# Reciprocal roots of a gated-attention and mixture-of-experts block: ten linked VectorE operations or one GpSimd power

## The chip, the core and the metric

The kernel runs on one core of one Trainium2 chip. A core has five engines that run their own instruction streams and meet through semaphores: TensorE (PE in the profile; its weight loads are shown apart as PEld), VectorE (DVE), ScalarE (ACT), GpSimd (POOL) and SyncE (SP). The metric is the device time of one execution in microseconds (us), as a median over runs; lower is better.

## What is computed

One adaptive-layernorm transformer layer over 4 x 1024 tokens of width 128. The parts with a reciprocal root are three: the first and second layernorm, the norm of every head's key (16 heads of 8), and the layernorm of the attention's output. Cut from the reference:

```python
def _layernorm(x, axis=-1, eps=1e-05):
    m = jnp.mean(x, axis=axis, keepdims=True)
    v = jnp.var(x, axis=axis, keepdims=True)
    return (x - m) / jnp.sqrt(v + eps)

# attention (h is the modulated first norm)
q = _silu(x @ Wq.T); k = _silu(x @ Wk.T); v = _silu(x @ Wv.T)
f = jax.nn.log_sigmoid(x @ Wf.T)
k = k / jnp.maximum(jnp.linalg.norm(k, axis=-1, keepdims=True), EPS_NORM)
# per token: S = exp(f) * S + k (outer) v ; o = q . S
o = o * gate
var = jnp.mean(xc * xc, axis=-1, keepdims=True)
o = xc / jnp.sqrt(var + EPS_LN) * ln_w
# whole layer
h = _layernorm(x) * (1 + ca) + sa
x = x + ga * attention(h)
h = _layernorm(x) * (1 + cb) + sb
x = x + gb * ffn(h)     # 2 shared experts, and 2 of 8 chosen per token
```

## The kernel before

Every engine's instruction stream is written out by hand. The 4096 tokens are worked in NB = 8 blocks of TB = 512, each four tiles of 128 tokens. A `first_period`, seven `period(i)` and a `drain` form a pipeline: in period i, block i is scanned, block i+1 is projected, block i-1 gets its attention output, block i-2 its second norm, router and first shared-expert product, and block i-3 the rest of the shared experts and the scatter of its rows to the experts' regions in DRAM. After the drain come 71 tiles of routed rows (about 300 to 410 us of the span) and the weighted sum.

What stands around the change, engine by engine:

- DVE carries the recurrence: for each of 8 value positions v a product `update` (line 1500) into PSUM and a `scan` (line 1513) over 512 tokens. Between them stand the statistics, the router's choice (`choose`, `mark`, `targets`), the products of the experts and, once per period, `roots`.
- `roots(n, a, z, ...)` (lines 1543 to 1552) takes the reciprocal root of up to 92 columns at once: 64 head norms of block i+1 (`clamp_norms`, line 1534), 4 output variances of block i-1 (`o_variance`, line 1541), 4 second-norm variances of block i-2 (`variance_2`, line 1590) and, in the first two calls, first-norm variances of later blocks. `rsqrt` (lines 63 to 76) does it in ten operations from a bit trick and two polynomial steps; `Chain` makes each one wait for the one before it.
- Who waits for `roots`: `offset_2` (line 1594), and through it ACT's `normalise_x2` (line 999) and PE's transposes (line 643) of block i-2; ACT's `widen_norms` (line 992), and through it the keys of block i+1 (`normalise_k`, line 1563); DVE's `residual` (line 1571), and through it `statistics_2`.
- The first two blocks' first norms take their roots in `statistics_1` at the start (lines 1385 to 1393).
- POOL works its stream in order: `query` (line 1221, seven products a block), the low halves of split operands (`split_h`, `split_v`, `split_h2`, lines 1204, 1209, 1214; `split_w13`, line 1263), `gain_w2` (line 1271, four products, in period 2), and eight indirect DMAs a block (`scatter`, line 1243). An operation that waits holds up all that stand behind it.

Of the kernel before, what the change touches and what calls it, by code (L numbers as in the profile page):

```python
# [36 lines left out]
P = 128  # L37
# [25 lines left out]
def rsqrt(dve, link, y, x, t, s):  # L63


    link(dve.tensor_scalar(t.bitcast(I32), x.bitcast(I32), 1, None, ALU.logical_shift_right))
    link(dve.tensor_scalar(y.bitcast(I32), t.bitcast(I32), -1, RSQRT_SEED, ALU.mult, ALU.add))
    link(dve.tensor_tensor(t, x, y, ALU.mult))
    link(dve.scalar_tensor_tensor(t, t, -0.5, y, ALU.mult, ALU.mult))
    link(dve.scalar_tensor_tensor(y, t, 1.5, y, ALU.add, ALU.mult))  # L70

    link(dve.tensor_tensor(t, x, y, ALU.mult))
    link(dve.tensor_tensor(t, t, y, ALU.mult))
    link(dve.tensor_scalar(s, t, 0.375, -1.25, ALU.mult, ALU.add))
    link(dve.tensor_tensor(t, t, s, ALU.mult))
    link(dve.scalar_tensor_tensor(y, t, 1.875, y, ALU.add, ALU.mult))


RSQRT_STEPS = 10
# [7 lines left out]
def build(nc, x, cmod, attw, wg12, w13T, w2T, bias, consts, ids, tiles, pads, H, out):  # L87
# [28 lines left out]
    with ExitStack() as ctx:  # L116
# [55 lines left out]
        tmp1 = sb("tmp1", [P, NB * NT])  # L172
# [16 lines left out]
        rtmp = sb("rtmp", [P, NSQ + NLATE])  # L189
# [76 lines left out]
        x_sq, t_sq, lg, pos, found, mu = parts(ybank, NSQ + NLATE, NSQ + NLATE, NT * NEXP, (NT + 1) * NEXP, NT * 8, NT)  # L266
        x_sq_end, t_sq_end, mu_end = parts(obank, NSQ, NSQ, NT)
# [18 lines left out]
        s_st1 = sem("s_st1")  # L286
        s_xn1 = sem("s_xn1")
# [27 lines left out]
        s_rs = sem("s_rs")  # L315
        s_x2 = sem("s_x2")
# [185 lines left out]
        def _(pe):  # L502
# [57 lines left out]
            def k_norms(b):  # L560
                wait(pe, s_ksq, b + 1)
                wait(pe, s_rs, RSQRT_STEPS * b)
                wait(pe, s_tgt, TGT_STEPS * (b - 3))
                wait(pe, s_var2, b - 2)
# [51 lines left out]
            def means(b, chains, routed):  # L616


                sq, _, mean = squares(b)
                wait(pe, s_og, b + 1)  # L620
                if b < NB - 1:
                    wait(pe, s_rs, RSQRT_STEPS * chains)
                    wait(pe, s_var2, b)
                    wait(pe, s_tgt, TGT_STEPS * (b - 1))
                    wait(pe, s_rt, RT_STEPS * routed)
# [3 lines left out]
                for t in range(NT):  # L629
                    ins = pe.matmul(sq[:, NT * H + t:NT * H + t + 1], oc_sq[:, t * P:(t + 1) * P], mean_col[:, :],  # L630
# [1283 lines left out]
```

## Time and profile before

| what | value |
|---|---|
| time, median of 3 runs | 443.28 us (440.53 to 445.61) |
| profiled execution, span from first to last instruction | 437.4 us |
| PE matmul busy | 388.6 us (89%) |
| DVE busy | 335.5 us (77%) |
| POOL busy | 287.1 us (66%) |
| ACT busy | 202.1 us (46%) |

For the profiled execution the page gives the span and no device time; the 5.9 us between 437.4 and the median 443.28 lie around the span and between executions. The shares are means over stages with different limits: DVE is at nine tenths or more from about 44 to 200 us and far lower after that, so the stages are read one by one below. A PE that is shown as busy may still be waiting a little between matmuls, since their ends are modelled. Times that stand in square brackets in a timeline row are the engine's idle time before that row and what ended it.

### The profile page before, as it was taken

The numbers are of one execution on the slowest core, as the hardware profiler recorded it, in microseconds if no ns is written. First come the engines' busy times: TensorE is split into PE (matmuls) and PEld (weight loads), VectorE is DVE, ScalarE is ACT, GpSimd is POOL, SyncE is SP. The second block draws the span as 40 slices with busy tenths as digits, with TensorE's granted clock in tenths as the row PEclk, the third lists the DMA queues.
The fourth block names the chain that finished last, engine by engine and source line by source line (L and its number), as shares of the span: only waits on it lengthen the run. The fifth ranks groups of instructions, "written<-read, shape, count | busy, mean of one in ns | idle before, by whom it ended". The sixth has DMA issues, their size and how long they took to land. (4 is left out here: it accounts for less than half of the span.)

```text
span 437.4 us, 8655 instructions
## 1 busy us (share of the span) xinstructions
PE 388.6 (89%) x2288; PEld 299.5 (68%) x2288; DVE 335.5 (77%) x987; ACT 202.1 (46%) x505; POOL 287.1 (66%) x354
## 2 busy tenths in 40 slices
PE   8967797669999999999987887888998998999885
PEld 4554373358687786877756666776887887888475
DVE  6778999996999999999999875544665665666545
ACT  4444334453656366453623344324554554555630
POOL 0145564877688887887868868662876878588600
PEclk9999989986999999999999899899999999999999
DMA  8800011000010000100001011132333333232197
GB/s 250 298 1 0 0 51 48 24 25 2 6 38 6 21 30 1 39 12 20 26 6 32 19 38 42 42 81 64 93 90 88 87 87 92 72 89 74 52 352 209
DMA packets 27808, 28.50 MB, mean 65 GB/s; under 512 B 4458, under 2 KB 21746, under 8 KB 27618
## 3 DMA queue, kind: packets, MB, share of 16 engines
q1 hardware_dynamic: 23442, 19.07, 15.0%
q0 software_dynamic: 4320, 8.89, 6.2%
q8 instruction: 20, 0.33, 0.3%
q14 instruction: 26, 0.21, 0.2%
HBM read 16.97 MB, written 12.03 MB: 66 GB/s over the span
## 5 line engine op out<-in xcount | busy, mean ns | idle before, releaser
L1221 POOL TENSOR_TENSOR qS<-S,qT 128x512 f32<-128x512 f32 x56 | 74.5, 1331 | 13.0 <-DVE S L1513 12.6
L1370 POOL DMA_INDIRECT y_dram<-S x71 | 70.7, 996 | 18.2 <-issue 16.6
L1243 POOL DMA_INDIRECT h_dram<-h,target_i x56 | 56.1, 1002 | 15.4 <-issue 15.0
L1785 DVE COPY qS<-ff 128x256 f32<-128x256 f32 x71 | 30.1, 424 | 41.7 <-PE ff L868 41.7
L1500 DVE TENSOR_TENSOR at<-at,khat 128x512 f32<-128x512 f32 x64 | 43.9, 689 | 3.7 <-PE at L584 2.9
L1170 ACT ACTIVATE S<-ff 128x256 f32<-128x256 f32 x71 | 27.2, 384 | 34.4 <-PE ff L861 34.4
L1513 DVE TENSOR_TENSOR_SCAN S<-decay,S,at 128x512 f32<-128x512 f32 x32 | 40.7, 1273 | 0.6
L1513 DVE TENSOR_TENSOR_SCAN S<-decay,at 128x512 f32<-128x512 f32 x32 | 38.7, 1212 | 0.6
L583 PE MATMUL at<-vT_hi,spread_v 128*128 128x512 f32 x64 | 31.5, 492 | 8.0 <-DVE S L1513 6.4
L859 PE MATMUL ff<-w_hi,vT_lo 128*128 x71 | 34.3, 483 | 3.2 <-issue 3.2
L1035 ACT ACTIVATE work<-ff 128x512 f32<-128x512 f32 x32 | 19.0, 594 | 38.2 <-PE ff L507 36.5
L1778 DVE TENSOR_TENSOR decay<-ff,S 128x256 f32<-128x256 f32 x71 | 29.4, 414 | 1.1 <-ACT S L1170 1.1
L505 PE MATMUL ff<-h2T_hi,w_hi 128*128 128x512 f32 x64 | 28.7, 448 | 1.1 <-issue 0.5
L583 PEld LDWEIGHTS at<-vT_hi,spread_v 128*128 128x128 f32 x64 | 12.7, 198 | 22.5 <-DVE S L1513 15.0
L860 PE MATMUL ff<-w_hi,vT_hi 128*128 x71 | 28.0, 394 | 0.0
L861 PE MATMUL ff<-w_lo,vT_hi 128*128 x71 | 28.0, 394 | 0.0
L1640 DVE TENSOR_TENSOR work<-ff,work 128x512 f32<-128x512 f32 x28 | 19.3, 688 | 10.5 <-ACT work L1035 10.1
L868 PE MATMUL ff<-consts_sb,decay 128*128 128x128 f32 x142 | 27.0, 272 | 0.0
L584 PE MATMUL at<-vT_lo,spread_v 128*128 128x512 f32 x64 | 26.7, 416 | 0.0
L507 PE MATMUL ff<-h2T_hi,w_lo 128*128 128x512 f32 x64 | 26.4, 412 | 0.0
L506 PE MATMUL ff<-h2T_lo,w_hi 128*128 128x512 f32 x64 | 26.3, 410 | 0.0
L1771 DVE TENSOR_TENSOR vT_lo<-at,vT_hi 128x128 fp32r<-128x128 f32 x71 | 19.9, 280 | 5.5 <-ACT vT_hi L1164 5.4
(272 smaller groups left out, 1037.3 us busy)
## 6 DMA issues: line engine op xcount, KB each, us to landing
S<-h_dram SPq DMA_DIRECT2D x71, 64.5 KB, 1.9
xall<-in_x SPq DMA_DIRECT2D x8, 256.0 KB, 5.4
work<-in_w13T SPq DMA_DIRECT2D x8, 256.0 KB, 2.7
w_hi<-y_dram SPq DMA_DIRECT2D x8, 256.0 KB, 5.3
w_lo<-y_dram SPq DMA_DIRECT2D x8, 256.0 KB, 5.7
out<-xall SPq DMA_DIRECT2D x8, 256.0 KB, 2.9
w_sb<-in_w2T SPq DMA_DIRECT2D x1, 1280.0 KB, 7.3
y_dram<-S POOLq DMA_INDIRECT x71, 2.3
```

Of the source, the lines that this page charges most:

```text
L505: pe.matmul(dst, w_hi, h_hi, start=True, stop=False)
L583: pe.matmul(at[half(v)][:, :], spread_v[:, v, :], vT_hi[:, :], start=True, stop=False)
L859: pe.matmul(ff[u % 2][:, :], t_lo[:, u % RING, :], w_hi[:, w], start=True, stop=False)
L860: pe.matmul(ff[u % 2][:, :], t_hi[:, u % RING, :], w_hi[:, w], start=False, stop=False)
L861: pe.matmul(ff[u % 2][:, :], t_hi[:, u % RING, :], w_lo[:, w], start=False, stop=True).then_inc(s_tf1, 1)
L1221: pool.tensor_tensor(qS[:, v, :], S[:, v, :], qT[:, b % 2, :], ALU.mult).then_inc(s_qS, 1)
L1243: pool.indirect_dma_start(out=h_dram[:, :], out_offset=bass.IndirectOffsetOnAxis(ap=target_i[:, b % 2, k, t:t + 1], axis=0), in_=token_row ...
L1370: pool.indirect_dma_start(out=y_dram[:, :], out_offset=bass.IndirectOffsetOnAxis(ap=rows[:, u, P:P + 1].bitcast(I32), axis=0), in_=y_sb[:, ...
L1500: dve.tensor_tensor(at[half(v)][:, :], at[half(v)][:, :], khat[:, b % 2, :], ALU.mult).then_inc(s_upd[half(v)], 1)
L1513: dve.tensor_tensor_scan(S[:, v, :], decay[:, b % 2, :], at[half(v)][:, :], before_it, ALU.mult, ALU.add) \
L1778: dve.tensor_tensor(t_G[:, u % RING, :], ff[u % 2][:, HID:2 * HID], t_silu[:, u % 2, :], ALU.mult) \
L1785: dve.tensor_copy(t_GT[:, u % RING, :], ff[2 + u % 2][:, 0:HID]).then_inc(s_tGT, 1)
```

## The change

The ten operations of `rsqrt` become one GpSimd `tensor_tensor` with the operation `pow`, against a tile `powers` filled with -0.5. POOL reads no PSUM tile in this kernel, so the values are first written to a new SBUF tile `sq` by the DVE operations that clamp or add the epsilon (they wrote to PSUM in place before). `roots` moves from DVE's stream to POOL's, behind `query(i, 2)`. `offset_2` moves too and becomes two POOL operations, `negate_mean` ahead of the root and a product behind it. DVE's `residual` and, in the first periods, `late_offsets` move behind the next `update` and `scan`. In the drain one scatter moves behind `split_h2(b)`. Waits of PE on the chain's semaphore become waits on the operations that now release PSUM.

```diff
-def rsqrt(dve, link, y, x, t, s):
-    link(dve.tensor_scalar(t.bitcast(I32), x.bitcast(I32), 1, None, ALU.logical_shift_right))
...
-    link(dve.scalar_tensor_tensor(y, t, 1.875, y, ALU.add, ALU.mult))
+def rsqrt(pool, y, x, powers):
+
+    return pool.tensor_tensor(y, x, powers, ALU.pow)
...
+            def roots_1(n, a, z):
+
+                pool.wait_ge(s_var1, n + 1)
+                rsqrt(pool, rstd1[:, a:z], var1[:, a:z], powers[:, 0:z - a]).then_inc(s_root1, 1)
+
+            def roots(n, a, z, norms, ovars, vars2):
...
+                rsqrt(pool, rsq[:, a:z], sq[:, a:z], powers[:, a:z]).then_inc(s_rs, 1)
...
+            def negate_mean(b):
...
+                pool.tensor_tensor(nmean2[:, :], mv2[:, :, 0], minus[:, :], ALU.mult).then_inc(s_nmean2, 1)
+
+            def offset_2(b, chains):
...
+                pool.tensor_tensor(nmr2[:, :], nmean2[:, :], rstd2[:, :], ALU.mult).then_inc(s_st2, 1)
...
             def clamp_norms(b):
                 wait(dve, s_n2, b + 1)
-                wait(dve, s_musq, b - 1)
-                dve.tensor_scalar(x_sq[:, 0:NT * H], x_sq[:, 0:NT * H], 1e-24, None, ALU.max).then_inc(s_n2c, 1)
+                wait(dve, s_rs, b)
+                dve.tensor_scalar(sq[:, 0:NT * H], x_sq[:, 0:NT * H], 1e-24, None, ALU.max).then_inc(s_n2c, 1)
...
             def residual(b):
                 wait(dve, s_out, b + 1)
+                wait(dve, s_rs, b + 3 + (b == NB - 1))
...
-                roots(i + 1, 0, NSQ + (NLATE if i == 1 else 0), min(i + 2, NB), i, i - 1)
-                if i == 1:
-                    late_offsets(3 * NT, NB * NT)
-                on(offset_2, i - 2)
-                on(residual, i - 1)
                 on(update, i, 4)
                 on(scan, i, 4)
+                if i == 1:
+                    late_offsets(2, 3 * NT, NB * NT)
+                on(residual, i - 1)
```

DVE in period 4, from the last scan ahead of the roots on (`at` is the PSUM product, `S` the scanned state, `ybank` and `sq` hold the squares, `rsq` the roots). Before:

```order
L1513 SCALAR_TENSOR_TENSOR S<-decay,at 128x512
L1541 SCALAR_TENSOR_TENSOR ybank<-ybank,mean_sq 128x4
L1534 TENSOR_SCALAR ybank<-ybank 128x64
L66 TENSOR_SCALAR ybank<-ybank 128x72
L67 TENSOR_SCALAR rsq<-ybank 128x72
L68 TENSOR_TENSOR ybank<-ybank,rsq 128x72
L69 SCALAR_TENSOR_TENSOR ybank<-ybank,rsq 128x72
L70 SCALAR_TENSOR_TENSOR rsq<-ybank,rsq 128x72
```

After:

```order
L1565 SCALAR_TENSOR_TENSOR S<-decay,at 128x512
L1594 SCALAR_TENSOR_TENSOR sq<-ybank,mean_sq 128x4
L1586 TENSOR_SCALAR sq<-ybank 128x64
L1552 TENSOR_TENSOR at<-at,khat 128x512
L1565 SCALAR_TENSOR_TENSOR S<-decay,at 128x512
L1615 SCALAR_TENSOR_TENSOR xall<-ff,rsq,xall 128x128 x4
L1552 TENSOR_TENSOR at<-at,khat 128x512
L1565 SCALAR_TENSOR_TENSOR S<-decay,at 128x512
```

The ten rows and the offset are gone, and the four rows of `residual` stand one update and one scan later.

POOL at the same place of a full period, from `number_rows` on (`h_dram` rows are the scatters). Before:

```order
L1232 COPY h<-ids_sb 128x8
L1240 TENSOR_TENSOR carrier<-consts_sb 128x1
L1243 DMA h_dram<-h,target_i 34816x129 x2
L1221 TENSOR_TENSOR qS<-S,qT 128x512
L1243 DMA h_dram<-h,target_i 34816x129
L1221 TENSOR_TENSOR qS<-S,qT 128x512
L1243 DMA h_dram<-h,target_i 34816x129
L1221 TENSOR_TENSOR qS<-S,qT 128x512
L1243 DMA h_dram<-h,target_i 34816x129 x3
L1214 TENSOR_TENSOR h2T_lo<-work,h2T_hi 128x512
```

After:

```order
L1238 DMA h_dram<-h,target_i 34816x129
L1216 TENSOR_TENSOR qS<-S,qT 128x512
L1292 TENSOR_TENSOR nmean<-mv,minus 128x4
L65 TENSOR_TENSOR rsq<-sq,powers 128x72
L1299 TENSOR_TENSOR nmr<-nmean,rsq 128x4
L1238 DMA h_dram<-h,target_i 34816x129
L1216 TENSOR_TENSOR qS<-S,qT 128x512
L1238 DMA h_dram<-h,target_i 34816x129 x3
L1209 TENSOR_TENSOR h2T_lo<-work,h2T_hi 128x512
```

Three operations stand between `query(i, 2)` and the fourth scatter, so four scatters, a query and `split_h2` are behind them.

POOL at the start of the program, from its last fill of zeros on (`ISA` is a row without operands). Before:

```order
L1274 MEMSET gather_v 128x64
L1279 COPY gather_v<-consts_sb 128x16 x2
L1209 ISA
L1209 TENSOR_TENSOR vT_lo<-vT,vT_hi 128x512
L1204 TENSOR_TENSOR hT_lo<-hT,hT_hi 128x512
```

After:

```order
L1303 MEMSET gather_v 128x64
L65 ISA
L65 TENSOR_TENSOR rstd<-var,powers 128x4
L1310 COPY gather_v<-consts_sb 128x16 x2
L65 TENSOR_TENSOR rstd<-var,powers 128x4
L65 TENSOR_TENSOR rsq<-sq,powers 128x64
L1204 TENSOR_TENSOR vT_lo<-vT,vT_hi 128x512
```

The ISA row stood behind the two copies and ahead of the first two-input operation; it still does the latter, but that is now the first root of the program.

## Rows read from the trace of the kernel before

**Rows 1.** Windows view by stage; columns are named in its first line.
```profile
core 0: us, PE busy (x) PEld busy (x) DVE busy (x) ACT busy (x) POOL busy (x), PEclk, DMA share, GB/s
0.00:17.60 17.60, 15.37 (x37) 9.05 (x38) 10.61 (x55) 7.10 (x12) 0.91 (x7) 1.00 0.96 298
34.00:63.00 29.00, 23.47 (x105) 13.39 (x104) 27.85 (x61) 10.18 (x20) 17.15 (x13) 0.97 0.06 18
63.00:94.50 31.50, 23.55 (x107) 13.76 (x105) 29.91 (x87) 14.17 (x28) 19.16 (x15) 0.98 0.13 34
94.50:122.58 28.08, 25.89 (x133) 19.67 (x133) 23.55 (x61) 14.63 (x29) 20.73 (x23) 0.82 0.02 6
...
150.69:178.60 27.91, 27.34 (x175) 21.12 (x173) 26.37 (x74) 15.71 (x31) 23.17 (x25) 1.00 0.06 20
```
**Rows 2.** Waits view, PEld, 122.58 to 206.5 us: total us, times, longest us.
```profile
PEld at L583 <- DVE S L1513: 4.1, 8, 0.8
```
**Rows 3.** Waits view, POOL, 122.58 to 206.5 us, waits for other engines.
```profile
POOL hT_lo L1204 <- ACT hT_hi L940: 3.9, 3, 1.3
POOL qS L1221 <- DVE S L1513: 2.2, 3, 0.7
POOL h2T_lo L1214 <- ACT h2T_hi L1015: 1.2, 3, 0.4
```
**Rows 4.** Timeline, DVE, one period's roots: start us, us, operation.
```profile
150.69 0.22 DVE L1534 TENSOR_SCALAR ybank<-ybank 128x64 f32<-128x64 f32 x1
150.95 0.24 DVE L66 TENSOR_SCALAR ybank<-ybank 128x72 int32<-128x72 int32 x1
...
153.40 0.23 DVE L76 SCALAR_TENSOR_TENSOR rsq<-ybank,rsq 128x72 f32<-128x72 f32 x1
153.67 0.53 DVE L1594 SCALAR_TENSOR_TENSOR nmr<-mv,rsq 128x4 f32<-128x4 f32 x1
...
155.16 0.68 DVE L1500 TENSOR_TENSOR at<-at,khat 128x512 f32<-128x512 f32 x1
155.87 1.22 DVE L1513 TENSOR_TENSOR_SCAN S<-decay,at 128x512 f32<-128x512 f32 x1
```
**Rows 5.** Lines view, POOL: two-input operations of two widths.
```profile
L1221 POOL TENSOR_TENSOR qS<-S,qT 128x512 f32<-128x512 f32 x56 | 74.5, 1331 | 13.0 <-DVE S L1513 12.6
...
L1251 POOL TENSOR_TENSOR dif<-top 128x4 f32<-128x4 f32 x8 | 1.6, 196 | 1.1 <-DVE top L1605 1.1
```
**Rows 6.** Timeline, POOL, `query(i, 2)` of the same period.
```profile
150.38 1.31 POOL L1221 TENSOR_TENSOR qS<-S,qT 128x512 f32<-128x512 f32 x1
```
**Rows 7.** Timeline, DVE, roots of the first period, first and last of ten.
```profile
35.37 0.24 DVE L66 TENSOR_SCALAR ybank<-ybank 128x76 int32<-128x76 int32 x1
...
37.86 0.24 DVE L76 SCALAR_TENSOR_TENSOR rsq<-ybank,rsq 128x76 f32<-128x76 f32 x1
```
**Rows 8.** Timeline, POOL, period 2: around `gain_w2`.
```profile
93.29 1.26 POOL L1263 TENSOR_TENSOR w_lo<-work,w_hi 128x512 fp32r<-128x512 f32 x1 [2.15 <-ACT w_hi L1051]
...
100.66 1.29 POOL L1214 TENSOR_TENSOR h2T_lo<-work,h2T_hi 128x512 fp32r<-128x512 f32 x1
```
**Rows 9.** Timeline, all engines, the start.
```profile
5.10 0.17 DVE L66 TENSOR_SCALAR tmp<-var 128x4 int32<-128x4 int32 x1
...
7.09 0.16 DVE L1392 SCALAR_TENSOR_TENSOR nmr<-mv,rstd 128x4 f32<-128x4 f32 x1
...
20.43 1.26 POOL L1209 TENSOR_TENSOR vT_lo<-vT,vT_hi 128x512 fp32r<-128x512 f32 x1 [10.66 <-ACT vT_hi L968]
20.52 1.46 DVE L1557 COPY rn_wide<-rsq 128x512 f32<-128x512 f32 x1
```
**Rows 10.** Timeline, POOL, the first operation of the drain.
```profile
246.88 1.27 POOL L1221 TENSOR_TENSOR qS<-S,qT 128x512 f32<-128x512 f32 x1
```
**Rows 11.** Waits view, POOL, 246.8 to 292 us: the longest two.
```profile
POOL h2T_lo L1214 <- ACT h2T_hi L1015: 1.5, 1, 1.5
POOL dif L1251 <- DVE top L1605: 1.1, 1, 1.1
```

More of the change, by code:

```diff
@@ L315, in build @@
         s_rs = sem("s_rs")
+        s_power = sem("s_power")
+        s_var1 = sem("s_var1")
+        s_root1 = sem("s_root1")
+        s_nmean2 = sem("s_nmean2")
         s_x2 = sem("s_x2")
@@ L561, in k_norms @@
                 wait(pe, s_ksq, b + 1)
-                wait(pe, s_rs, RSQRT_STEPS * b)
+                wait(pe, s_n2c, b)
+                wait(pe, s_varc, b - 2)
                 wait(pe, s_tgt, TGT_STEPS * (b - 3))
-                wait(pe, s_var2, b - 2)
                 for t in range(NT):
@@ L649, in logits @@
                 if b < NB - 1:
-                    wait(pe, s_rs, RSQRT_STEPS * (b + 4))
-                    wait(pe, s_var2, b + 1)
+                    wait(pe, s_n2c, min(b + 4, NB))
+                    wait(pe, s_varc, min(b + 2, NB - 1))
                 else:
@@ L986, in square_mean @@
                 wait(act, s_varc, b)
-                act.activation(mean_sq[:, :], squares(b)[2], ACT.Square).then_inc(s_musq, 1)
+                act.activation(mean_sq[:, :], squares(b)[1], ACT.Square).then_inc(s_musq, 1)
             def widen_norms(b):
-                wait(act, s_rs, RSQRT_STEPS * (b + 1))
+                wait(act, s_rs, b + 1)
                 wait(act, s_rnT, b)
@@ L1280, in _ @@
             ins.then_inc(s_gather, 1)
+            roots_1(1, NT, 2 * NT)
+            roots(0, 0, NT * H, 1, 0, 0)
             split_v(0)
@@ L1287, in first_period @@
                 query(0, 2)
+                roots(1, 0, NSQ + NT, 2, 0, -1)
                 query(0, 3)
@@ L1312, in period @@
                 on(query, i, 2)
+                on(negate_mean, i - 2)
+                roots(i + 1, 0, NSQ + (NLATE if i == 1 else 0), min(i + 2, NB), i, i - 1)
+                on(offset_2, i - 2, i + 2)
                 if i == 1:
@@ L1331, in period @@
                 on(split_v, i + 1)
+                if i == NB - 1:
+                    negate_mean(i - 1)
+                    roots(i + 2, NT * H + NT, NSQ, NB, i, i)
+                    offset_2(i - 1, i + 3)
             def drain():
@@ L1340, in drain @@
                 score_gap(b)
-                scatter(a, 4, 8)
+                scatter(a, 4, 6)
+                roots(NB + 2, NT * H, NT * H + NT, NB, NB, c)
+                scatter(a, 6, 8)
                 weights(b)
                 number_rows(b)
-                scatter(b, 0, 1)
                 split_h2(b)
-                scatter(b, 1, 5)
+                negate_mean(c)
+                roots(NB + 3, NT * H + NT, NSQ, NB, NB, NB)
+                offset_2(c, NB + 4)
+                scatter(b, 0, 5)
                 add_shared(a)
@@ L1399, in late_variances, with late_offsets @@
                 link(ins)
-                link(dve.tensor_scalar(x_sq[:, NSQ:NSQ + b - a], mv[:, a:b, 1], 1e-5, None, ALU.add))
-            def late_offsets(a, b):
+                wait(dve, s_rs, 2 * n - 2)
+                dve.tensor_scalar(sq[:, NSQ:NSQ + b - a], mv[:, a:b, 1], 1e-5, None, ALU.add).then_inc(s_late, 1)
+            def late_offsets(n, a, b):
+                dve.wait_ge(s_rs, n + 1)
                 root = rsq[:, NSQ:NSQ + b - a]
@@ L1589, in variance_2 @@
                 wait(dve, s_st, 2 * b + 2)
[L1590 to L1594 removed]
+                wait(dve, s_rs, b + 3)
+                dve.tensor_scalar(sq[:, NT * H + NT:NSQ], mv2[:, :, 1], 1e-5, None, ALU.add).then_inc(s_var2, 1)
             def choose(b):
@@ L1642, in _ @@
             clamp_norms(0)
-            roots(0, 0, NT * H, 1, 0, 0)
             widen_norms(0)
@@ L1737, in drain @@
                 o_variance(c)
-                roots(NB + 2, NT * H, NT * H + NT, NB, NB, c)
                 targets(b)
@@ L1743, in drain @@
                 variance_2(c)
-                roots(NB + 3, NT * H + NT, NSQ, NB, NB, NB)
-                offset_2(c)
                 product(b, 0)
```

95 lines of the change are left out of this document (48 added, 47 removed).

## Prediction

> **What bounds the kernel now.** I read the windows view first, cut by stage [rows 1]. From 34 to 94 us, periods 0 and 1, DVE is busy 27.85 of 29.00 and 29.91 of 31.50 us and PE about four fifths: DVE is the bound. In period 2 (94.5 to 122.6) DVE is busy only 23.55 of 28.08. Each of the four full periods from 122.6 to 234.3 us looks like the one shown: DVE 26.37 of 27.91, PE 27.34, POOL 23.17. There three engines are close to full, so relief of one is worth what the next leaves. From 291 us on no root is left, and I expect nothing of that stage.
>
> How much each of the other two leaves is read from the waits. PE's weight loads wait for DVE's scans 4.1 us in three full periods [rows 2], so with a faster DVE the period can fall by about 1.4 us until PE itself is the limit: 26.5 us. POOL waits for other engines 3.9 + 2.2 + 1.2 = 7.3 us in the same three [rows 3], 2.4 a period: its own work is 27.9 - 2.4 = 25.5 us.
>
> **What goes.** One call on DVE, read in the timeline: the ten linked operations run from 150.95 to 153.63 and the offset ends at 154.20 [rows 4], so 2.7 us of roots and 0.5 of offset leave DVE in every full period. The call of the first period is as long, 35.37 to 38.10 [rows 7]. DVE's limit falls from about 27.4 to 24.2 us, and it is no longer the bound.
>
> **What comes, and its price X.** POOL gets one power over 72 columns and two small products per full period. The small ones cost 0.2 us each, as the 128x4 subtraction does [rows 5]; with a gap between them I take 0.55 us. A power is in no row. Lower end: it costs what any two-input operation of POOL costs. 512 columns take 1.331 us and 4 take 0.196 [rows 5], so a column is 2.2 ns and 72 columns 0.34 us. Upper end: POOL must do by program what the ten operations did, at ten times that, 3.4 us. Nothing excludes either, so I take the geometric middle, X = 1.1 us for 72 columns (1.0 for 64, 1.35 for 92, 0.25 for 4), a few passes of arithmetic under one fixed cost. All that follows hangs on X.
>
> The Trainium skill speaks against the move: "GPSIMD Engine Reference", section "Elementwise — side-by-side cycle accounting", gives 2.6 cycles an element for a two-input operation on GpSimd against about one on VectorE, and concludes that elementwise work belongs on VectorE. As an estimate from that page, ten passes at 2.6 cycles of 1.2 GHz over 72 columns are 1.6 us; by it the sum below would lose some 3 us of its gain. Its rate is that of the rows, 2.2 ns a column [rows 5]; how many passes a power is, no row here shows.
>
> **Step by step, X = 1.1.**
>
> Start. The first chain runs from 5.10 to 7.09 us [rows 9]; 0.25 us on POOL and two hand-overs would save 1.5, but the loads fill that stage (DMA share 0.96 [rows 1]) and much of it would wait for them: I credit 0.5. The third call (64 columns) ends in DVE's widening copy at 20.52, which takes 1.46 us beside POOL's 1.26 us at 20.43 [rows 9]. Now `split_v` stands behind the root on POOL and the copy runs ahead of it; PE has filler work until about 21.5, so again 0.5. Together -1.0 us.
>
> The ISA row ahead of the first two-input operation moves into this stage as well. Before, it stood where POOL was idle for 10.66 us [rows 9], so its cost was hidden and is between nothing and 10.66 us. It now stands where about 4 us are free before the first root can start. I take it as hidden; at 10.66 the first root would be 4.7 us late. "GPSIMD Engine Reference", section "Instruction dispatch", of the Trainium skill puts about 6 us on the first use of freshly loaded code; by that the first chain would end 0.2 us late instead of gaining 0.5.
>
> Period 0. DVE is the bound and loses 2.7 us of work; the wait for the root moves behind an update and a scan, 0.68 + 1.22 = 1.9 us of cover [rows 4], more than X. The queries behind the root on POOL start about an X later, in a stretch where POOL is busy 17.15 of 29.00 us [rows 1]. I credit 2.5. Period 1: the same, with 92 columns, and 1.35 is still under the cover: 2.5. Together -5.0 us.
>
> Period 2. DVE is not the bound there. POOL waits 2.15 us for ACT until 93.29 and then runs without a break through four gain products to `split_h2` at 100.66 [rows 8], on which the first expert product waits. The root goes into those 2.15 us, and what follows starts when it did: 0.
>
> Full periods. POOL's own work becomes 25.5 + 0.55 + 1.1 = 27.15 us, PE's limit is 26.5, DVE's 24.2. POOL is the new bound, at 0.75 less than 27.9; four such periods: -3.0 us. What is late next: the root starts when POOL ends `query(i, 2)`, at 151.69 [rows 6], 0.8 us after the clamp's end on DVE at 150.91 [rows 4], and ends with its offset near 153.4, 0.8 ahead of the old 154.20. So ACT's norm and PE's transposes get their data no later, while four scatters, a query and `split_h2` are 1.65 us later on POOL, and the expert products of PE behind them.
>
> End. In period 7 the root of 4 columns stands ahead of POOL's drain. It waits for `variance_2`, which DVE issues just ahead of the roots that start at 249.65 in its own timeline; POOL was at its next query at 246.88 [rows 10] and now starts it near 250.2, 3.3 us late. Two more small roots and an offset add 0.9. Against these 4.2 us stand POOL's waits in the drain, 1.5 and 1.1 [rows 11] and about 1.5 in shorter ones. The roots themselves come 1.5 us sooner each, but POOL's scatters end the stage. I charge 1.0 us.
>
> Sum: -1.0 - 5.0 + 0 - 3.0 + 1.0 = -8.0 us. The profiled span 437.4 would be 429.4, and the median 443.3 becomes **435.3 us**; the 5.9 us between the two are taken as unchanged.
>
> **Both ends of X.** At 0.34 POOL's own work is 26.4 and PE's limit of 26.5 takes over: 4 x 1.4 = 5.6; start and early periods 6.8, end -0.8: -11.6, 431.7 us. At 3.4 the start loses 0.8 (the 64-column root ends later than the ten operations did, and `split_v` is behind it); period 0 gains 1.0 and period 1 0.4, since the root outlasts its cover; period 2 loses 1.5; each full period is 25.5 + 0.55 + 3.4 = 29.45, 1.55 more than now, 6.2 in all; the end loses 3.5: +10.6, 453.9 us. The sum is zero near X = 2.3: period 0 2.3, period 1 1.6, start 0.5, against 0.6 in period 2, 4 x 0.45 and 2.0 at the end.
>
> **Rivals.**
> (a) The power is cheap, X below 0.7: 430 to 433 us. For it: it is one operation of a kind that POOL runs at 2.2 ns a column. Against: more arithmetic than a product.
> (b) The gain stays in the early periods. X between 1.6 and 2.8, or PE and POOL so entangled that a full period stays at 27.9, or the ISA row's cost in the open: 439 to 447, say 440. For it: PE at 27.34 of 27.91 busy [rows 1] may hide no more than it shows. With all of the 10.66 us in the open, the start is 4.2 worse than my sum before any of it is taken up, 440 as well.
> (c) POOL becomes a worse bound than DVE was: slower than before. The mechanism is X itself, in POOL's stream between `query(i, 2)` and the scatters; it decides from X = 2.3 on, and every further microsecond costs one in each full period and as much in period 7. At 3.4 the time is 454; at 6 us, if a power goes through long scalar code, 4 x 4.15 and some 10 in the other stages, near 470. For it: POOL leaves only 2.4 us a period [rows 3]. Against: ten plain passes fit into 3.4.
> (d) POOL's operations slow DVE through what they share. DVE's offset takes 0.53 where 0.16 is its time alone, and the copy at 20.52 1.46 us, both beside a POOL operation [rows 4, 9]. During the root DVE runs an update and a scan, which read PSUM and show no such growth beside POOL's query, so I charge nothing. "GPSIMD Engine Reference", section "Specifications", says that the two engines share an SBUF interface and that operations with two SBUF inputs contend; the rows agree, and the change takes one such operation off DVE.
>
> **Chances and range.** My forecast (X 0.7 to 1.6, 433 to 438.5): 0.35. (a) 0.18. (b) 0.22, of which most within 1%. (c) 0.25, of which 0.12 beyond 454. About 1% (4.4 us) is what a measurement of this kernel can tell from no change: the three runs shown spread by 0.6% either way. Faster: forecast and (a), 0.53; same 0.22; slower 0.25. The forecast's own range is 433 to 439. For eight in ten both signs must be in: 430 to 454, from the cheap end to the upper bound of X, leaves out some 0.05 below and 0.12 above.
>
> **What would show it.** The duration of the power at 72 columns, above all, and at 4 and 92 for its slope. In full periods: waits of POOL gone, waits of DVE for POOL at `residual` under 0.5 us, the period near 27.1. In periods 0 and 1: 2.5 us less each between clamps. At the start: first root over before 7.1 us. In the drain: POOL waiting for `variance_2`, and the last scatter no more than 1 us later against the drain's start. A power over 2 us, a first root after 8 us, or full periods still at 27.9 would prove me wrong, each in its own step.

## The result and the profile after

| | time, median of 4 | profiled span | granted clock | PE busy | DVE busy | POOL busy |
|---|---|---|---|---|---|---|
| before | 442.7 us (440.53 to 445.61) | 437.4 us | 0.976 | 388.6 us | 335.5 us | 287.1 us |
| after | 552.35 us (550.02 to 554.09) | 550.7 us | 0.869 | 415.1 us | 310.3 us | 405.2 us |

After over before is 1.2515 (1.2445 to 1.2585): slower by a quarter, and 98 us above the upper end of the range. DVE lost 25 us of work, about as foreseen; POOL gained 118. (Ratios here leave disturbed executions out, so they need not be the quotient of the medians beside them; the profiled executions of e8 and e12 are disturbed ones, 453.54 and 441.76 us, and of the four executions of e2 only 485.70 and 488.71 us are not. Around the span lie 1.8 us, 552.52 against 550.7 in the profiled execution of after, not the 5.9 that the prediction took.)

The price X comes first. Lines view of after, POOL, all powers (count | total us, mean ns of one | idle before them):

```profile
L65 POOL TENSOR_TENSOR rsq<-sq,powers 128x72 f32<-128x72 f32 x6 | 71.4, 11902 | 0.0
L65 POOL TENSOR_TENSOR rsq<-sq,powers 128x92 f32<-128x92 f32 x1 | 15.0, 15032 | 3.0 <-DVE sq L1449 3.0
L65 POOL TENSOR_TENSOR rsq<-sq,powers 128x76 f32<-128x76 f32 x1 | 12.5, 12513 | 2.3 <-DVE sq L1449 2.3
L65 POOL TENSOR_TENSOR rsq<-sq,powers 128x64 f32<-128x64 f32 x1 | 10.6, 10552 | 2.8 <-DVE sq L1586 2.8
L65 POOL TENSOR_TENSOR rsq<-sq,powers 128x4 f32<-128x4 f32 x3 | 3.1, 1046 | 2.9 <-issue 2.7 <-POOL nmean L1292 0.2
L65 POOL TENSOR_TENSOR rstd<-var,powers 128x4 f32<-128x4 f32 x2 | 2.1, 1030 | 9.0 <-DVE var L1435 9.0
```

A power of 72 columns takes 11.90 us, where the forecast took 1.1 and bounded it by 3.4. From 4 to 64 columns it grows by (10.55 - 1.05) / 60 = 0.158 us a column, some 70 times the 2.2 ns of a product [rows 5]; what does not depend on the columns is about 0.4 us. The nine wide calls (64 columns and more) sum to 71.4 + 15.0 + 12.5 + 10.6 = 109.5 us, and the time grew by 109.7. That the two agree so closely is chance in part: single stages below grew by less or by more than their power.

Windows view of after, cut at DVE's clamps; the last row runs from the clamp in period 6 through period 7 and the drain to the last scatter:

```profile
18.59:43.94 25.35, 15.73 (x60) 10.93 (x61) 10.07 (x19) 7.80 (x15) 16.77 (x6) 0.87 0.04 17
43.94:83.87 39.93, 25.36 (x108) 14.51 (x107) 28.23 (x52) 11.35 (x22) 29.84 (x14) 0.83 0.05 13
83.87:126.05 42.18, 23.50 (x98) 13.49 (x99) 26.71 (x64) 12.73 (x26) 32.73 (x15) 0.80 0.09 26
126.05:167.75 41.70, 27.36 (x140) 20.46 (x138) 23.97 (x63) 15.75 (x31) 34.20 (x27) 0.75 0.01 4
209.04:250.14 41.10, 31.00 (x175) 24.20 (x173) 23.87 (x63) 15.71 (x31) 35.51 (x28) 0.83 0.04 14
291.07:403.79 112.72, 82.91 (x456) 65.76 (x454) 58.15 (x191) 32.28 (x66) 93.41 (x90) 0.80 0.09 27
```

Two rows of before, cut at its own clamps ([rows 1] are cut at other places; there its period 1 ends at 94.5, behind the clamp at 91.04): period 2, and from the clamp in period 6 to the last scatter.

```profile
91.04:122.58 31.54, 27.31 (x140) 20.48 (x138) 26.63 (x74) 15.74 (x31) 22.05 (x24) 0.84 0.02 5
206.47:290.83 84.36, 73.16 (x456) 58.22 (x454) 67.27 (x245) 32.28 (x66) 65.01 (x76) 0.96 0.12 35
```

Set beside the same stretches of before, every stage with a wide root is longer by about one power (the one from the clamp in period 6 on holds two), and the routed tiles are as they were (before, after, and two kernels of the experiments, one profiled execution of each; us):

| stage, clamp to clamp | before | after | product for power (e1) | one operation on DVE (e12) |
|---|---|---|---|---|
| start to first clamp | 17.62 | 18.59 | 16.54 | 17.41 |
| to the second clamp | 15.90 | 25.35 | 15.66 | 14.63 |
| period 0 | 29.52 | 39.93 | 27.59 | 28.50 |
| period 1 | 28.00 | 42.18 | 26.64 | 26.52 |
| period 2 | 31.54 | 41.70 | 31.63 | 32.90 |
| three full periods (3 to 5), mean | 27.96 | 41.11 | 28.38 | 27.87 |
| clamp in period 6 to the last scatter | 84.36 | 112.72 | 89.12 | 89.68 |
| rest | 146.57 | 146.91 | 146.97 | 146.75 |

Where a full period of after waits: waits view, 167.75 to 291.07 us, three periods (total us, times, longest), answering [rows 2, 3].

```profile
ACT xn L994 <- POOL nmr L1299: 34.0, 3, 11.5
DVE xall L1615 <- POOL rsq L65: 31.5, 3, 10.6
PE ff L638 <- ACT xn L994: 29.1, 3, 9.9
POOL hT_lo L1199 <- ACT hT_hi L935: 7.4, 3, 2.5
```

Three engines stand behind one instruction. The timeline of after shows it in one period, POOL first (start us, us; before: [rows 4, 6]), then DVE's residual, ACT's norm and PE:

```profile
208.76 1.29 POOL L1216 TENSOR_TENSOR qS<-S,qT 128x512 f32<-128x512 f32 x1
210.16 11.90 POOL L65 TENSOR_TENSOR rsq<-sq,powers 128x72 f32<-128x72 f32 x1
222.14 0.20 POOL L1299 TENSOR_TENSOR nmr<-nmean,rsq 128x4 f32<-128x4 f32 x1
...
222.18 1.13 DVE L1615 SCALAR_TENSOR_TENSOR xall<-ff,rsq,xall 128x128 f32<-128x128 f32 x4 [10.43 <-POOL rsq L65]
...
222.38 1.65 ACT L994 ACTIVATE xn<-xall,nmr,rsq 128x128 f32<-128x128 f32 x4 [11.23 <-POOL nmr L1299]
...
224.08 1.11 PE L638 MATMUL ff<-consts_sb,xn 128*128 128x128 f32 x4 [9.59 <-ACT xn L994]
...
231.84 0.63 PE L501 MATMUL ff<-h2T_lo,w_hi 128*128 128x512 f32 x1
232.26 0.52 PE L502 MATMUL ff<-h2T_hi,w_lo 128*128 128x512 f32 x1
232.62 0.39 PE L500 MATMUL ff<-hT_hi,watt_hi 128*128 128x512 f32 x1
232.85 0.39 PE L501 MATMUL ff<-hT_lo,watt_hi 128*128 128x512 f32 x1
```

The cover of an update and a scan, 1.9 us, is spent at 211.75; the root ends at 222.06. After its wait of 9.59 us PE works at the lower of its two clock levels until 232.3: matmuls of 512 columns start 0.42 to 0.43 us apart there, and 0.23 apart behind it. That is the granted clock of 0.83 in the windows, against 1.00 in the same stage before.

### The profile page after: what moved, and what is told of

Read it like the earlier page. It is cut to its first block and busy times, and to the rows that moved or that the text cites. A ratio compares the mean times of both kernels' runs of the same rounds, so it can differ in the third digit from the quotient of the medians.

```text
span 550.7 us, 8573 instructions
## 1 busy us (share of the span) xinstructions
PE 415.1 (75%) x2288; PEld 319.1 (58%) x2288; DVE 310.3 (56%) x839; ACT 202.4 (37%) x505; POOL 405.2 (74%) x386
## 2 busy tenths in 40 slices
DMA packets 27808, 28.50 MB, mean 52 GB/s; under 512 B 4458, under 2 KB 21746, under 8 KB 27618
## 5 line engine op out<-in xcount | busy, mean ns | idle before, releaser
L65 POOL TENSOR_TENSOR rsq<-sq,powers 128x72 f32<-128x72 f32 (+4 forms) x12 | 112.6, 9387 | 11.0 <-DVE sq L1449 5.3
L578 PE MATMUL at<-vT_hi,spread_v 128*128 128x512 f32 x64 | 34.3, 536 | 31.1 <-DVE S L1565 30.7
L638 PE MATMUL ff<-consts_sb,xn 128*128 128x128 f32 x28 | 7.8, 434 | 65.1 <-ACT xn L994 65.1
L1816 DVE COPY qS<-ff 128x256 f32<-128x256 f32 x71 | 30.1, 425 | 41.4 <-PE ff L863 41.4
L638 PEld LDWEIGHTS ff<-consts_sb,xn 128*128 128x128 f32 x28 | 5.0, 217 | 68.6 <-ACT xn L994 68.6
L1615 DVE SCALAR_TENSOR_TENSOR xall<-ff,rsq,xall 128x128 f32<-128x128 f32 x28 | 7.9, 343 | 63.1 <-POOL rsq L65 63.1
L578 PEld LDWEIGHTS at<-vT_hi,spread_v 128*128 128x128 f32 x64 | 14.4, 225 | 44.4 <-DVE S L1565 36.5
L1165 ACT ACTIVATE S<-ff 128x256 f32<-128x256 f32 x71 | 27.3, 384 | 34.3 <-PE ff L856 34.3
L994 ACT ACTIVATE xn<-xall,nmr,rsq 128x128 f32<-128x128 f32 x32 | 13.2, 482 | 70.9 <-POOL nmr L1299 70.8
L500 PE MATMUL ff<-h2T_hi,w_hi 128*128 128x512 f32 x64 | 31.8, 497 | 2.8 <-issue 1.7
L501 PE MATMUL ff<-h2T_lo,w_hi 128*128 128x512 f32 x64 | 29.7, 463 | 0.0
L502 PE MATMUL ff<-h2T_hi,w_lo 128*128 128x512 f32 x64 | 28.9, 451 | 0.0
```

The costliest lines, as they stand in the source:

```text
L65: return pool.tensor_tensor(y, x, powers, ALU.pow)
L500: pe.matmul(dst, w_hi, h_hi, start=True, stop=False)
L501: pe.matmul(dst, w_hi, h_lo, start=False, stop=False)
L578: pe.matmul(at[half(v)][:, :], spread_v[:, v, :], vT_hi[:, :], start=True, stop=False)
L1816: dve.tensor_copy(t_GT[:, u % RING, :], ff[2 + u % 2][:, 0:HID]).then_inc(s_tGT, 1)
```

## Experiments

A full period in what follows is one of the three whose mean stands in the table.

**The price taken away (e1).** In after, one word:

```diff
-    return pool.tensor_tensor(y, x, powers, ALU.pow)
+    return pool.tensor_tensor(y, x, powers, ALU.mult)
```

> The changed kernel with one word different: the operation of every root is a product with the same tile instead of a power, so the roots' values are left out (each becomes -0.5 times its input). Order, waits, reads and writes stay. Theory A (everything in the forecast's sum but the price of the power was right): the 72-column operation takes about 0.34 us as any two-input operation of POOL, and the time is that of the sum's lower end, 431.7 us (430 to 434). Theory B (the moved order costs by itself: the longer stream of POOL, the hand-overs between DVE and POOL, the later residual): 439 to 447 us or more, with waits for POOL's roots still in the trace.

Measured: 440.83 us, 1.0016 (0.9968 to 1.0064) of before; 72 columns take 0.338 us, the lower bound. So all of the loss hangs on the power. But theory A falls too: with X at its cheapest the sum gave 431.7, and no gain can be told. The time is theory B's, though no wait for POOL's root is left in the full periods. The table shows where the gain went in the profiled execution: the stages up to period 1 come in 1.1 + 0.2 + 1.9 + 1.4 = 4.6 us sooner, and that goes again as 0.1 in period 2, 0.4 in each full period and 4.8 at the end. That the moved order makes the 4.8 is not shown: e12 below, where nothing moved, has as long an end in its one profiled execution. Waits view of e1, full periods, 118 to 203 us:

```profile
DVE at L1552 <- PE at L579: 8.3, 9, 1.8
...
PE ff L500 <- POOL h2T_lo L1209: 1.9, 3, 0.8
```

In the same three periods of before the first of these waits was 1.6 us and the second was not there. DVE's freed time turned into waiting for PE; and POOL's low half of h2, behind three more small operations, now comes too late for PE's first expert product (0.6 us a period).

**The ten operations taken away, nothing moved (e12).** In before:

```diff
 def rsqrt(dve, link, y, x, t, s):
-    link(dve.tensor_scalar(t.bitcast(I32), x.bitcast(I32), 1, None, ALU.logical_shift_right))
...
-    link(dve.scalar_tensor_tensor(y, t, 1.875, y, ALU.add, ALU.mult))
-RSQRT_STEPS = 10
+    link(dve.tensor_scalar(y, x, 0.5, None, ALU.mult))
+RSQRT_STEPS = 1
```

> The kernel before, with one product on VectorE in place of the ten linked operations of each reciprocal root (the roots' values are left out); nothing moves to POOL and the order stays. DVE loses 9 x 0.27 = 2.4 us in every period, at no price elsewhere. Theory A (as the forecast had it: DVE bounds periods 0 and 1, and in full periods PE's own limit is 26.5 us, 1.4 below the period): start 0.5 to 1, periods 0 and 1 about 2.3 each, four full periods 1.4 each: 443 - 11 = 432 us (430 to 434). Theory B (PE was as much the limit as DVE, since its 27.3 of 27.9 us are all work and the waits were those of weight loads): full periods fall by 0.4 us at most, the early ones by 2: 437 to 440 us, and DVE's idle time shows waits for PE in place of the roots.

Measured: 439.22 us, 0.9932 (0.9878 to 0.9985). Theory B. Windows view of e12, two full periods:

```profile
119.96:147.79 27.83, 27.18 (x173) 21.15 (x173) 24.78 (x66) 15.60 (x31) 23.39 (x25) 1.00 0.07 21
147.79:175.74 27.95, 27.28 (x175) 21.30 (x173) 24.44 (x65) 15.59 (x31) 23.20 (x25) 1.00 0.06 20
```

Waits view of e12, 119.96 to 203.57 us, three full periods (1.6 us in before):

```profile
DVE at L1489 <- PE at L573: 5.9, 6, 1.6
```

DVE is busy about 2 us less than before, waits for PE instead, and the period is the same 27.9: PE, at 27.2, is the limit. Roots at a tenth of their operations, with the order kept, are worth 0.7% (0.15 to 1.2%), won in the stages up to period 1 (by the table 0.2 + 1.3 + 1.0 + 1.5 us). More than that a move of the roots alone could hardly bring here; what another order might bring besides, this run doesn't show.

**Doses of X (e2, e3).** In after, ten linked products for each power, or the power on half of the columns:

```diff
+    link(pool.tensor_tensor(y, x, powers, ALU.mult))
+    for _ in range(8):
+        link(pool.tensor_tensor(y, y, powers, ALU.mult))
+    return pool.tensor_tensor(y, y, powers, ALU.mult)
```
```diff
+    n = y.shape[-1] // 2
+    pool.tensor_tensor(y[:, 0:n], x[:, 0:n], powers[:, 0:n], ALU.pow)
+    return pool.tensor_tensor(y[:, n:], x[:, n:], powers[:, n:], ALU.mult)
```

> The changed kernel with ten linked products on POOL in place of each power; the roots' values are left out. This is the upper end of the forecast's bounds, made real. Theory A (only the duration X of POOL's root decides): X comes to 10 x (0.34 + a hand-over of about 0.06) = 4.0 us for 72 columns, and by the forecast's sum, which is zero at 2.3 and +10.6 us at 3.4, the time is about 460 us (455 to 466). Theory B (the loss of the changed kernel comes from the power as a kind of operation, which holds up more than its own duration on POOL): ten cheap operations lose little, 435 to 447 us.

> The changed kernel with the power on the first half of the columns of each root and a product on the second half, whose roots are left out. With 0.160 us a column, X is 36 x 0.160 + 0.35 + 0.25 = 6.4 us for 72 columns. Theory A (every microsecond of POOL over the free time of a period is paid in full, and nothing else is): a full period becomes 25.5 + 0.55 + 6.4 = 32.45, 4.55 more than before, in four full periods, and about as much in each of four other stages: 443 + 36 = 479 us. Theory B (in the changed kernel PE's idle time also lowers its clock, and that part shrinks with the stall): on the line between 431.7 us at X = 0.34 and 552.4 at 11.9, 495 us, with a granted clock between 0.869 and 0.976.

Measured: 491.68 us for e2 (485.7 to 498.5; 487.2 as the mean of 485.70 and 488.71) and 507.94 us for e3, 1.153 (1.140 to 1.166). Timeline of e2, POOL, first, middle eight (merged) and last of the ten; the chain takes 174.37 - 170.30 = 4.07 us:

```profile
170.30 0.33 POOL L65 TENSOR_TENSOR rsq<-sq,powers 128x72 f32<-128x72 f32 x1
170.71 3.24 POOL L67 TENSOR_TENSOR rsq<-rsq,powers 128x72 f32<-128x72 f32 x8
174.03 0.34 POOL L68 TENSOR_TENSOR rsq<-rsq,powers 128x72 f32<-128x72 f32 x1
```

In e3 72 columns take 6.16 + 0.25 = 6.4 us. So it is the duration that counts, not the kind: cheap operations that add up to 4 us lose some 46 us against e1. Both came out above their theory A (460 and 479), e3 above its theory B as well:

| X, 72 columns | 0.34 (e1) | 4.07 (e2) | 6.4 (e3) | 11.9 (after) |
|---|---|---|---|---|
| time, us | 440.8 | 487.2 | 507.9 | 552.4 |
| POOL busy in the profile, us | 293.6 | 329.9 | 352.8 | 405.2 |
| full period, mean, us | 28.4 | 34.1 | 36.7 | 41.1 |
| POOL's own 25.5 + 0.55 + X | 26.4 | 30.1 | 32.5 | 38.0 |
| granted clock of the execution | 0.957 | 0.891 | 0.888 | 0.869 |

From e3 to after the time grows by 44.4 us for 5.5 us of X, 8.1 for each: nearly the number of wide calls, nine. Below that it is steeper (12 for each from e1 to e2). From X = 4.07 on a full period exceeds POOL's own work, by 4 us in the middle and 3 in after (at 0.34 PE is the limit, not POOL). Most of the excess is one wait. Waits view, three full periods, of e2 and of e3; in after it was 7.4, in before 3.9:

```profile
POOL hT_lo L1203 <- ACT hT_hi L939: 10.3, 3, 4.5
POOL hT_lo L1201 <- ACT hT_hi L937: 10.7, 3, 5.5
```

**The exponent (e_exp1).** In after:

```diff
-            pool.memset(powers[:, :], -0.5).then_inc(s_power, 1)
+            pool.memset(powers[:, :], 1.0).then_inc(s_power, 1)
```

> The changed kernel with +1.0 in place of -0.5 in the tile of exponents: each power returns its input, so the roots are left out. Theory A (the power goes through one fixed program whatever the numbers): 72 columns take 11.9 us as before and the time stays at 552 us. Theory B (the time depends on the exponent, since a whole one can be had by products): the 72 columns take less than half, and the time falls below 500 us.

Measured, one execution: 551.09 us, and 11.904 us for 72 columns. Theory A: the price is the same for the two exponents tried.

**The power cut in two (e7).** In after; a `head_roots` takes columns 0 to 63 and has a semaphore of its own, and ACT's `widen_norms` moves behind `take_q`. Cut from the edit:

```diff
-                roots(i + 1, 0, NSQ + (NLATE if i == 1 else 0), min(i + 2, NB), i, i - 1)
+                roots(i + 1, NT * H, NSQ + (NLATE if i == 1 else 0), i, i - 1)
...
                 on(split_h2, i - 2)
+                if 1 < i < NB - 1:
+                    head_roots(i + 1)
```

> The changed kernel, roots and all, with each wide power cut in two: first the 8 columns that the second norm and the residual wait for (28 and 8 in the first periods), and, behind split_h2, the 64 columns of the head norms; period 7, which has no head norms left to do, leaves that second part out. By 0.160 us a column the parts take 1.65 and 10.55 us. Theory A (the total of POOL's stream sets the period): a full period is 25.5 + 0.55 + 1.65 + 10.55 = 38.3 us against 41.1 measured, period 7 loses 10 more: 552 - 14 - 10 = 528 us (522 to 534). Theory B (the wait of PE and DVE behind the long power sets the period): that wait falls from 9.6 to about 1 us, full periods go back to 28 to 31 us, and the time falls under 490 us.

Measured: 532.96 us, 1.2119 (1.2029 to 1.2208). Theory A, 5 us off. Windows and waits of e7, full periods:

```profile
200.03:239.59 39.56, 29.53 (x175) 22.98 (x173) 26.95 (x63) 15.93 (x31) 35.77 (x29) 0.87 0.04 14
```
```profile
ACT rn_wide L988 <- POOL rsq L65: 19.3, 3, 7.4
PE ff L570 <- ACT rn_wide L988: 19.6, 3, 7.6
```

The residual and the second norm no longer wait, and the period is still 39.6, not 28 to 31. The wait has moved to the head norms: PE's transposes of them wait 19.6 us in three periods. POOL itself waits only 1.4 us for DVE and ACT in this period (0.8 for a scan, 0.6 for `hT_hi`), so its own work, about 38.2, is the bound. With that total no other place in POOL's stream would bring the period back to 28.

**Fillers on PE (e5, e5b, e5c).** In after, idle products ahead of the wait; ten alone (e5), twelve and four (e5b), ten and two (e5c). The edit of e5c:

```diff
+                if i > 2:
+                    keep_busy(ff[1], 10)
                 on(transpose_x2, i - 2, i)
...
+                if i > 2:
+                    keep_busy(ff[1], 2)
                 on(up, i - 2, 0)
```

> The changed kernel with ten idle products of PE (512 columns, result not used) put where PE waits about 9.6 us for the second norm, in periods 3 to 7. Theory A (part of the loss is that PE comes out of the wait at the low clock and runs some 8 us at half pace, which delays the next period's operands to POOL by 2.4 us): the clock stays up, POOL's wait for hT_hi goes, and the time is 540 us (535 to 545). Theory B (POOL's stream alone sets the period and PE's pace is hidden): 552 us as before (549 to 555), with the higher clock in the trace all the same.

> The changed kernel with idle products of PE at two places of periods 3 to 7: twelve ahead of the second norm's transposes and four ahead of the first expert product, where PE waited another 2.3 us for POOL's split_h2 when there were ten at the first place alone (that run came out at 563.7 us, with periods of 44.3 us: the low clock had only moved behind this second wait). Theory A (the low clock behind the waits costs the period some 2 us, since PE's stretch from the expert product to the next block's transposes lies on the same loop as POOL's power): with the clock up in both stretches the full period is 38 to 39.5 us and the time 540 us (536 to 546). Theory B (fillers only delay PE's own work): 560 us or more.

> The changed kernel with idle products of PE sized to its two waits in periods 3 to 7: ten ahead of the second norm's transposes, two ahead of the first expert product (with twelve and four the clock was up, but the fillers ended 1.0 and 1.7 us after the data were there, and the full period stayed at 41.2 us). Theory A (the low clock behind the wait costs the period about 2 us, and only the surplus of fillers hid it): full periods of 38.7 to 39.7 us, and about 545 us (540 to 548). Theory B (the loop through POOL's power, its scatters, split_h2 and the next block's transposes is as long at either clock): 41 us and 551 to 556 us.

Measured: 563.72 (1.2775, 1.2709 to 1.2841), 558.55 and 556.98 us: none gained, and none came to its theory A (the ratio of e5c is 1.2643, 1.2513 to 1.2772, which meets that of after). Windows of e5, of e5b and of e5c, full periods:

```profile
206.47:250.76 44.29, 40.45 (x195) 28.70 (x193) 23.98 (x63) 15.71 (x31) 35.39 (x28) 0.88 0.04 13
```
```profile
209.33:250.65 41.32, 40.74 (x207) 27.47 (x205) 23.86 (x63) 15.71 (x31) 35.45 (x28) 1.00 0.04 14
```
```profile
167.17:209.72 42.55, 40.73 (x197) 27.61 (x197) 23.97 (x64) 15.71 (x31) 35.56 (x28) 0.92 0.04 14
209.72:249.67 39.95, 37.80 (x199) 25.77 (x197) 24.43 (x63) 15.71 (x31) 35.48 (x28) 1.00 0.05 14
```

In e5 the low clock only moved behind the next wait, 2.3 us for `h2T_lo`, and two of three full periods rose to 44.3 (the first took 41.4). In e5b the clock stayed up and nothing was won. Only the sized fillers of e5c bring periods of 39.95 and 39.8 at a clock of 1.00, 1.2 us below after; a third fell to 0.92 and took 42.55, and its last stage, from the clamp in period 6, is 4 us longer. In the period of 39.95 POOL's wait for `hT_hi` is 1.3 us, against 2.5 in after:

```profile
POOL hT_lo L1203 <- ACT hT_hi L939: 1.3, 1, 1.3
```

So, by these two periods, the low clock is worth about 1.2 us of the 13 by which a full period of after is longer. The rest is POOL's own work and its other waits.

**The offset alone (e6, e6c).** In before, for blocks 0 to 5, with the product behind `query(i, 3)` (e6, shown) or ahead of it (e6c); DVE's `on(offset_2, i - 2)` goes:

```diff
+                on(negate_mean, i - 2)
                 on(query, i, 2)
...
                 on(query, i, 3)
+                on(offset_2, i - 2)
```

> The kernel before with only the second part of the change: the second norm's offset of blocks 0 to 5 as two POOL products (the negated mean ahead of query(i, 2), the product behind query(i, 3)), the roots left on VectorE. Theory A (the offset is off the limits: 0.53 us less on DVE, 0.4 us more on POOL, which has 2.4 us free a period): within 1 us of before, 442 to 444. Theory B (the product stands behind a query that ends at about the time of the old offset, and PE's transposes wait for it): up to 0.7 us more in each of six periods, 445 to 448 us.

> The kernel before with the offset alone moved to POOL, as in the run of that kind, but with the product ahead of query(i, 3) in place of behind it, so that POOL waits for VectorE's root (about 1 us a period) and the offset comes when it is there. Theory A (the place of the product made the loss: the offset was late, by 2.8 us in period 2 above all, PE waited for it and fell to the low clock): back to the time of before, 440 to 445 us. Theory B (the late offset isn't the cause): 447 to 452 us again.

Measured: 450.95 us, 1.0258 (1.0194 to 1.0321), and 450.80 us, 1.0257 (1.0189 to 1.0325). Against the medians of all executions of before beside them, 444.29 and 444.22 us, both are 1.5% longer. The smaller half of the change, costed at 0.55 us of POOL's free time, is a loss by itself; e6 came out above both of its theories, and theory B of e6c holds: the place against the query is not the cause. The trace of e6c shows two things. In period 2 the product stands, as in e6, behind a `split_w13` that waits 4.2 us for ACT; PE's transposes come 7.6 us after the clamp, against 5.3 before. And a POOL that waits for the root is late with `split_h2`, as in e1; waits of PE in e6c, full periods, and the window of its last stage:

```profile
PE ff L509 <- POOL h2T_lo L1218: 2.5, 3, 0.9
```
```profile
212.91:303.63 90.72, 80.20 (x456) 64.07 (x454) 66.09 (x243) 32.36 (x66) 65.17 (x80) 0.87 0.12 33
```

The profiled execution of e6c is 12.6 us longer than that of before: 0.6 in each of the three full periods, which goes with that wait; 1.7 in period 2; 2.7 in periods 0 and 1, where nothing was moved; and 6.4 from the clamp in period 6 on, at a clock of 0.87 against 0.96. What lengthens the drain is not settled: apart from one new wait of 0.7 us for `h2T_lo` (and 0.6 in issue), no wait of PE there is longer, and e12, where nothing went to POOL, has a last stage of 89.68 us at 0.87 too. So that the offset costs is shown; of how, only the 0.6 us a period.

**Order (e9, e10).** In e1, `split_h2` one scatter earlier; in e10 the drain's scatter back as well:

```diff
-                on(scatter, i - 3, 4, 7)
+                on(scatter, i - 3, 4, 6)
                 on(split_h2, i - 2)
+                on(scatter, i - 3, 6, 7)
```

> The kernel with products in place of the powers (the roots' values are left out), and in every period one of POOL's scatters moved from ahead of split_h2 to behind it, so that split_h2 stands 1.3 us earlier. Theory A (with a root at no price, what eats the gain is that POOL's split_h2 comes 0.4 us later against PE's stream and holds the first expert product, 0.5 us a period and 2.3 us in period 7, after which PE runs at the low clock): that wait goes, 4 x 0.4 + 2 to 4 us come back, and the time is 437 us (434 to 439) against 441. Theory B (PE's stream is full whatever POOL does): 441 us, and PE's periods stay at 28.3.

> As the run with the earlier split_h2 (products in place of the powers, so the roots' values are left out), and in the drain the first scatter of block 6 back ahead of split_h2, where it stood before the change. Theory A (in the drain POOL then works where it otherwise waits 2.2 us for ACT, and the chain of scatters ends one scatter earlier): 1.3 us less than the run without it, 435 to 437 us. Theory B (the end of the drain is set elsewhere): the same time as without it.

Measured: 446.14 us (437.4 to 453.9), which tells nothing, and 443.48 us, 1.0013 (0.9953 to 1.0073). Waits of e10, full periods:

```profile
PE ff L500 <- DVE work L1683: 0.8, 3, 0.3
...
POOL qS L1216 <- DVE S L1567: 3.8, 3, 1.3
```

PE's wait for `h2T_lo` is gone, as theory A of e9 said, but the period stays at 28.4: PE waits for DVE's product instead (0.3 us a period), POOL more for the scans (3.8 against 2.2 in e1). That is theory B of e9; whether the drain's order matters can't be told, since e9 tells nothing. The profiled execution's period 2 took 37.95 us at a clock of 0.66, against 31.63 at 0.84 in e1, whose code for that period is the same: a single execution's stage can be some 6 us off without any change.

**Only the narrow roots (e8).** In before, the first norms' two roots as powers of 4 columns:

```diff
-                rsqrt(dve, link, rstd1[:, a:b], var1[:, a:b], tmp1[:, a:b], nmr1[:, a:b])
...
+                pool.tensor_tensor(rstd1[:, a:z], var1[:, a:z], powers[:, :], ALU.pow).then_inc(s_root1, 1)
```

> The kernel before with the power on POOL only where 4 columns are all there is and the start waits for them: the first norms' roots of blocks 0 and 1. A power of 4 columns took 1.03 us where the ten operations took 2.0 us. Theory A (the start is a chain through the first root): 1.0 us less at the start, 442.3 us, which this measurement can't tell from none. Theory B (the loads of the start end last): the first clamp on DVE comes no sooner than the loads let it, 443.3 us.

Measured: 445.30 us, 1.0009 (0.9937 to 1.0080). The power takes 1.04 us from 5.14 and the offset starts at 6.22, 0.9 sooner than [rows 9], but DVE's next operation then waits for the load of the constants until 7.20, as theory B had it. No difference that can be told.

## Why the prediction was wrong

**The price X, the step that failed.** "At ten times that, 3.4 us" was called an upper end, but it rested on nothing but the belief that POOL takes a root in about as many passes as DVE. Ten passes were then made real (e2): 4.07 us, already above the 3.4. The power takes 11.9, three times that. Rival (c) gave the mechanism and the place, POOL's stream between `query(i, 2)` and the scatters, and "every further microsecond costs one"; it named 6 us and 470, with 0.25 for the whole and 0.12 beyond 454. An unknown operation with no row had no upper bound from the rows, and the range should have said so.

The prediction's own formula with X = 11.9 gives a full period of 25.5 + 0.55 + 11.9 = 38.0; measured is 41.1. The 3.1 are in the step "waits of POOL gone", which failed as well: POOL still waits 2.5 us a period for `hT_hi` and 0.7 for a scan. The loop runs from POOL over ACT and PE back to POOL, and PE's stretch in it runs at the low clock, 1.2 us by e5c. In e2 and e3 the same wait is 3.4 and 3.6 us a period, and both times came out above their theories A: the sum would have fallen short of the loss even with the right X.

The page "GPSIMD Engine Reference" of the Trainium skill, section "Elementwise — side-by-side cycle accounting", gives about 2.6 cycles an element for a two-input operation. The trace agrees for products (2.2 ns a column) and not for the power (158 ns); the section's advice to keep elementwise work on VectorE is borne out (72 columns: 2.7 us on VectorE in ten operations, 11.9 on GpSimd in one).

**The gain, wrong by itself.** The 26.5 us for PE's limit were got by taking the waits of PE's weight loads [rows 2] off the period. Those overlap with matmuls: PE was busy 27.3 of 27.9, and e12 shows the same 27.9 with 2 us less on DVE. So full periods had nothing to give (27.9 in e12, 28.4 in e1), where the sum took -3.0 or -5.6 for four of them; rival (b), in which they stay at 27.9, was right in this. Periods 0 and 1 were sized 2.5 each: in e1 they gained 1.9 and 1.4, in e12 1.0 and 1.5. So even with X at its lower end 431.7 was out of reach: 440.8.

**What is late next.** The prediction named it (four scatters, a query and `split_h2` 1.65 us later on POOL, "and the expert products of PE behind them") and charged nothing. In e1, with only 1 us more in front, PE already waits 0.6 us a period for it. The end, charged with 1.0 (0.8 at the X of e1), was 4.8 longer in e1's profiled execution, at a clock of 0.90 against 0.96; the wait for `variance_2`, foreseen as 3.3 us, was 2.7. How much of the 4.8 the move makes stays open, as said at e1.

**The small products.** Costed by their duration, 0.55 us against 2.4 us of POOL's free time; e6 and e6c put the offset alone at 2.6% (1.5% by the medians of all executions). Where e6c shows it, in the full periods, it is not the operation's length that is paid but the wait of what stands behind it: `split_h2` is late, and PE waits for it.

**What held.** DVE's freed time; the place where POOL becomes the bound; nothing charged for slowing DVE while the power runs (a scan beside it takes 1.22 us as before); nothing on the routed tiles. At the start, the ISA row cost nothing that shows: timeline of after,

```profile
5.25 1.05 POOL L65 TENSOR_TENSOR rstd<-var,powers 128x4 f32<-128x4 f32 x1 [4.23 <-DVE var L1435]
...
6.34 0.16 DVE L1440 SCALAR_TENSOR_TENSOR nmr<-mv,rstd 128x4 f32<-128x4 f32 x1 [1.24 <-POOL rstd L65]
```

The first root is over before 7.1, as the list wanted. The 6 us that "GPSIMD Engine Reference", section "Instruction dispatch", of the Trainium skill puts on the first call to freshly loaded code do not show here: the root starts 4.2 us after POOL's last fill, as soon as its operand is there. Whether this call loads code at all, no run shows. But the first clamp came at 18.59 in after and between 15.40 and 18.96 in other kernels with the same first root, so the 0.5 us of gain can't be read.

## What to carry to other kernels

An operation that no row shows has no upper bound from neighbouring rows: measure it in a kernel of a few lines first, at the width that is needed, or let the range hold that it decides everything. Before moving work off an engine, take it away without putting it anywhere (as e12 does): that shows about what the move can bring at best, here 0.7%. And a busy share close to the period may be the limit itself: the waits of weight loads were no spare time of the matmuls here.

## What the runs showed of the hardware

- POOL's power: about 0.4 us and 0.16 us a column at 128 partitions, 1.05 us for 4 columns, 11.90 for 72, the same for exponents -0.5 and 1.0. Linked products of 72 columns follow each other every 0.41 us (e2).
- PE that comes out of a wait of some 10 us ran at half pace for 8 us (after, 224.1 to 232.3). Filling one wait moved the low clock to the next one and cost 3 us in two of three full periods (e5).
- Two DVE operations of 4 columns each took 1.22 and 1.18 us beside two-input products of POOL, about as long as those (the first of them takes 0.14 in e1); timeline of after, period 0, the first, just after a power:

```profile
58.48 1.26 POOL L1216 TENSOR_TENSOR qS<-S,qT 128x512 f32<-128x512 f32 x1
58.54 1.22 DVE L1455 COPY rstd<-rsq 128x4 f32<-128x4 f32 x1 [10.92 <-POOL rsq L65]
```

- With the same code, period 2 took 31.63 us at a clock of 0.84 (e1) and 37.95 at 0.66 (e10). Executions of before scatter from 437 to 455 us; how much of that lies in such stretches is not shown, since one execution of each kernel was profiled.
